# A decoder layer on one core: one norm instead of two in front of the cross layer, weights prepared two units a step, two copies on ScalarE, and the four-head norms' bias on VectorE

## The reference

```python
x = x + attn(_layernorm(x), Wqkv_w, Wqkv_b)        # 16 heads of 32, rotary, causal
x = x + xattn(_layernorm(x), ctx_2048, ...)        # self and cross, 16 heads of 128 each
x = x + ffn(_layernorm(x), w_gate_up, w_proj)      # ternary weights, silu(gate) * up, rms_norm
return x

def _layernorm(x, eps=1e-5):
    return (x - mean(x)) / sqrt(var(x) + eps)

def xattn(hidden, cond, ...):
    ln_out = _ln(hidden, ln_w, ln_b)               # (x - mu) * rsqrt(var + 1e-5) * w + b
    q  = _ln(fp8_linear(ln_out, wq),  qln_w, qln_b)    # norms over each head's 128
    k  = _ln(fp8_linear(ln_out, wk),  kln_w, kln_b)
    v  = fp8_linear(ln_out, wv)
    qx = _ln(fp8_linear(ln_out, wqx), qxln_w, qxln_b)
    kx, vx = split(cond @ w_kv_x.T);  kx = _ln(kx, kxln_w, kxln_b)
    cat = concat([gqa(q, k, v), gqa(qx, kx, vx)])      # softmax attention, 8 k/v groups
    return fp8_round(cat / proj_smooth) @ wproj.T * (proj_in_scale * proj_w_scale)
```

## Time and profile before

| | us | share of the span |
|---|---|---|
| median of 3 runs | 1264.98 | |
| the profiled execution | 1269.58 | |
| its span | 1267.8 | |
| PE busy, 6408 matmuls | 1196.8 | 94% |
| DVE busy | 947.8 | 75% |
| ACT busy | 811.6 | 64% |
| POOL busy | 608.8 | 48% |

### The profile page before, as it was taken

The page is one execution under the profiler, slowest core; times in us unless marked ns, Lnnn a source line. Parts: engine busy times, 40 slices in busy tenths (PEclk is TensorE's granted clock), DMA queues, the critical chain, the costliest instruction groups (busy, mean ns, idle before and its releaser), DMA issues.

```text
span 1267.8 us, 19453 instructions
## 1 busy us (share of the span) xinstructions
PE 1196.8 (94%) x6408; PEld 818.9 (65%) x6432; DVE 947.8 (75%) x2826; ACT 811.6 (64%) x2325; POOL 608.8 (48%) x722
## 2 busy tenths in 40 slices
PE   4999989789999999999999999999999998999998
PEld 2676666556677666676666777676677765555545
DVE  4669988999888887799999966657777877463341
ACT  4566558767877875676667765566787676652230
POOL 1728774654453454555555732124454534363370
PEclk9999889899999999999999999999999999899999
DMA  8211100012110221113233221041112100000000
GB/s 265 81 50 36 33 1 1 1 34 60 58 51 18 63 80 58 54 63 104 87 108 98 60 79 38 17 141 58 46 30 58 48 28 1 1 1 11 20 1 29
DMA packets 25461, 65.61 MB, mean 52 GB/s; under 512 B 2720, under 2 KB 8992, under 8 KB 25360
## 3 DMA queue, kind: packets, MB, share of 16 engines
q1 hardware_dynamic: 25088, 64.00, 16.4%
q10 hardware_dynamic: 272, 0.36, 0.1%
HBM read 59.37 MB, written 4.98 MB: 51 GB/s over the span
## 4 chain that ended last, share of the span: by engine, by line
PE 51%; DVE 26%; ACT 16%; POOL 4%; issue 2%; DMA 1%; SPq 0%; ACTq 0%; POOLq 0%
PE ps L869 10%; PE ps L1133 8%; PE ps L1066 7%; ACT big L799 5%; PE ps L859 5%; PE ps L1182 4%; PE ps L1028 3%; PE ps L961 3%; DVE big L412 3%; DVE big L981 2%; ACT big L964 2%; PE ps L993 2%; PE ps L500 2%; DVE big L654 2%; DVE big L240 2%
## 5 line engine op out<-in xcount | busy, mean ns | idle before, releaser
L869 PE MATMUL ps<-big 128*125 128x512 bf16 x1152 | 265.7, 380 | 0.1
L799 ACT ACTIVATE big<-ps,big 112x128 f32<-112x128 f32 (+1 forms) x512 | 192.4, 456 | 72.0 <-POOL big L429 69.6
L869 PEld LDWEIGHTS ps<-big 128*125 128x125 bf16 x1152 | 156.0, 137 | 80.7 <-issue 1.0
L428 POOL TENSOR_TENSOR big<-big 112x4 f32<-112x4 f32 (+1 forms) x128 | 39.2, 306 | 320.9 <-ACT big L423 320.8
L859 PE MATMUL ps<-big 128*112 128x512 bf16 x768 | 186.9, 387 | 5.2 <-ACT big L889 1.3
L658 POOL TENSOR_TENSOR big<-big 128x448 f32<-128x448 bf16 x96 | 103.6, 1080 | 110.2 <-DVE big L978 69.1
L859 PEld LDWEIGHTS ps<-big 128*112 128x112 bf16 x768 | 100.0, 132 | 68.6 <-issue 6.1
L981 DVE TENSOR_SCALAR big<-big 112x112 f32<-112x112 f32 (+1 forms) x256 | 132.7, 539 | 6.8
L412 DVE BATCH_NORM_STATS2 big<-ps 112x6 f32<-112x128 f32 (+1 forms) x512 | 113.3, 283 | 21.5 <-PE ps L869 19.4
L964 ACT ACTIVATE big<-ps,big 112x375 f32<-112x375 f32 x128 | 74.6, 583 | 83.9 <-DVE big L963 82.8
L1028 PE MATMUL ps<-big 125*128 125x224 f32 (+1 forms) x512 | 122.5, 362 | 4.2 <-DVE big L1010 3.4
(11 more groups left out here) (117 smaller groups left out, 2353.3 us busy)
## 6 DMA issues: line engine op xcount, KB each, us to landing
big<-in_ctx_t SPq DMA_DIRECT2D x32, 375.0 KB, 3.4
big<-in_w_s SPq DMA_DIRECT2D x16, 512.0 KB, 3.6
big<-in_w_p SPq DMA_DIRECT2D x16, 512.0 KB, 3.7
big<-in_w_x SPq DMA_DIRECT2D x16, 512.0 KB, 3.8
big<-in_w_g SPq DMA_DIRECT2D x16, 512.0 KB, 3.8
big<-in_w_d SPq DMA_DIRECT2D x8, 512.0 KB, 4.2
big<-in_w_a SPq DMA_DIRECT2D x8, 384.0 KB, 5.1
scr<-big SPq DMA_DIRECT2D x24, 128.0 KB, 1.7
```

What stands on the lines that cost most here:

```text
L799: t = act(lambda e, j=j: e.activation(z[0:rows, 128 * j:128 * j + 128], bk[0:rows, 128 * j:128 * j + 128], ACT.Identity, bias=rr[0:rows, 4 ...
L869: t = pe(lambda e, k=k, s=s, u=u, n=n: e.matmul(bk[0:CK, :], cT[:, s, k, CK * c:CK * c + CK], w[:, u, k, col:col + 512], start=n == 0, sto ...
```

## The change

Five edits:

- `l_1`, `l_1h` and their `ln_r` go. `l_0h` applies one scale that stands for both norms: the variance of the first norm's result is v/(v+e), so both together are (x - mean) / sqrt(v(1+e) + e*e), up to rounding (e = 1e-5). All later pieces of `l_` move one step forward.
- The 24 units of S0 are prepared two a step from step 4 on, so they end at step 15 instead of 27.
- `a_te` of q, and `a_s2e` of the second of four groups, go from DVE to ACT.
- The bias -mean*r of the four-head norms leaves POOL (two instructions) for DVE (one, `p_q`).
- `p_q` and `p_z` stand at the head of the next tick, lag 2, instead of inside tick 1.

```diff
-        def ln_rstd(s):
+        def ln_rstd(s, twice=False):
...
-            t = act(lambda e: e.activation(r, s["var"], ACT.Ln, bias=cf[0:rows, C_EPS:C_EPS + 1]), s["t"], t_c)
+            col, mul = (C_EPS2, 1.0 + EPS) if twice else (C_EPS, 1.0)
+            t = act(lambda e: e.activation(r, s["var"], ACT.Ln, bias=cf[0:rows, col:col + 1], scale=mul), s["t"], t_c)
...
-            tq = pool(lambda e: e.tensor_tensor(s["q"], s["mean"], r, ALU.mult), t)
-            s["tr"] = [t, pool(lambda e: e.tensor_scalar(s["q"], s["q"], -1.0, None, ALU.mult), tq)]
-            return s["i"], s["rr"], s["tr"]
+            s["te"] = t
+            return s["i"], s["rr"], None
...
+        def l_r(it):
+            it["rs"] = ln_rstd(it["st"], twice=True)
...
-            if j:
-                te = act(lambda e: e.activation(qT, src, ACT.Copy), t, of)
-            else:
-                te = dve(lambda e: e.tensor_copy(qT, src), t, of)
+            te = act(lambda e: e.activation(qT, src, ACT.Copy), t, of)
...
-            if g["c"] in (3,):
+            if g["c"] in (1, 3):
...
-        A_LEAD, A_Q, T0 = 10, 14, 34
+        A_LEAD, A_Q, T0 = 10, 13, 34
...
-                (lead + 7, ln_r),
-                (lead + 8, l_1),
-                (lead + 8, ln_r),
+                (lead + 7, l_r),
...
-                (lead + 10, l_2),
+                (lead + 9, l_2),
...
-                (lead + 8, l_1h),
...
+        def p_q(it):
+            if it["what"] != "v":
+                s = it["st"]
+                it["tr"] = [s["te"], dve(lambda e: e.scalar_tensor_tensor(
+                    s["q"], s["mean"], -1.0, s["r"], ALU.mult, ALU.mult), s["te"])]
...
+            if n >= 4:
+                next(s0prep, None)
...
-        order = [("p", 1, p_stats), ("p", 1, p_vhi), ("a", 3, t_s2), ("a", 0, t_s0), ("p", 1, p_rstd), ("a", 5, t_s4),
-                 ("p", 3, p_t), ("b", 6, b_4), ("b", 3, b_2), ("a", 1, t_s1), ("p", 1, p_z), ("a", 8, t_s6),
+        order = [("p", 2, p_q), ("p", 2, p_z), ("p", 1, p_stats), ("p", 1, p_vhi), ("a", 3, t_s2), ("a", 0, t_s0), ("p", 1, p_rstd), ("a", 5, t_s4),
+                 ("p", 3, p_t), ("b", 6, b_4), ("b", 3, b_2), ("a", 1, t_s1), ("a", 8, t_s6),
                  ("a", 4, t_s3), ("p", 0, p_mm), ("b", 2, b_m), ("b", 4, b_3), ("b", 1, b_1), ("b", 0, b_0)]
```

More of the change, by code:

```diff
@@ L29 @@
 V_WS, V_PW, V_PI, V_N = 64, 68, 69, 70
-C_ID, C_COSQ, C_SINQ, C_COSK, C_SINK, C_HALF, C_UNIT, C_EPS, C_N = (
-    0, 128, 160, 192, 224, 256, 260, 261, 262)
+C_ID, C_COSQ, C_SINQ, C_COSK, C_SINK, C_HALF, C_UNIT, C_EPS, C_EPS2, C_N = (
+    0, 128, 160, 192, 224, 256, 260, 261, 262, 263)
 K_ONE, K_DIAG, K_MASK, K_N = 0, 128, 240, 688
@@ L676, in l_0h @@
             it["l"] = (zi, z, th)
[L678 to L688, removed]
         def l_2(it):
@@ L746, in run_a @@
                 ("h", 3, a_s3),
-                (lead + 10, l_2),
[L748 to L751, removed]
+                (lead + 9, l_2),
+                (lead + 10, lambda it: l_q(it, (0,), False)),
+                (lead + 11, lambda it: l_q(it, (1,), False)),
+                (lead + 12, lambda it: l_q(it, (2,), False)),
+                (lead + 13, lambda it: l_q(it, (3,), True)),
                 (1, a_tr),
@@ L792, in p_rstd @@
                 si, rr, tr = ln_rstd(it["st"])
-                it.update(si=si, rr=rr, tr=tr)
+                it.update(si=si, rr=rr)
+        def p_q(it):
[3 more added lines that the diff above has]
+                    s["q"], s["mean"], -1.0, s["r"], ALU.mult, ALU.mult), s["te"])]
         def lnb_z(it):
@@ L1364, in _constants @@
     c[:, C_EPS] = EPS
+    c[:, C_EPS2] = EPS * EPS
     return c, d
```

## The result

| | before | after |
|---|---|---|
| median, us | 1265.59 (1264.97 to 1268.60) | 1331.27 (1328.77 to 1333.89) |
| span of the profiled execution | 1267.8 | 1327.0 |
| first cross projection on PE | 168.6 | 164.7 |
| first self scores | 214.6 | 203.5 |
| first context projection | 466.5 | 455.2 |

The changed kernel is slower by 66 us, four runs each: ratio 1.0507 [1.0482, 1.0531]. The forecast was 1251.5 with a range to 1264. From the first self scores to 489.9 us the changed kernel is 10 to 11 us ahead, about as forecast. Between the first cross-half scores and the last context projection it takes 627.2 us instead of 558.9. These 68 us, in the two cross halves, are the loss, and the forecast had charged nothing for them; less the 10 us won before, they make the 59 us by which the two profiled executions differ (the medians differ by 66).

A forecast was written before the change was run, and what follows sets the result against it. It took PE to bound the kernel in its pauseless stages and DVE from 95.04 to 174.01 us. +2.5 + 1 - 6.5 - 9.5 - 1 = -13.5 us gave 1256.1 profiled, 1251.5 median; range 1240 to 1264.

The forecast's parts named there:

- After 460: nothing: From 460 us on: no change, PE being the bound with 80 bias instructions of 0.3 us beside it; -2 to +3.
- L783 at 0.3 us: The new DVE bias instruction: 0.3 us each, taken near the lower end between 0.155 and 1.1.
- the bias meets POOL: Rival, to 460 us: L783 waits for POOL's quant instructions, 1.1 us each, 48 us on DVE; 1268.5 us, chance 0.10.
- Start, later by 2.5: 26 to 41 us: a second weight unit per step delays DVE's first bias addition and the rotary by 2.5; bounds 0.7 and 5.
- 38.50 to 88.37, later by 1: Twelve more weight units, 9 us of DVE, mostly covered by idle time: 1 us later; bounds 0 and 4.
- 88.37 to 177.56, earlier by 6.5: DVE loses about 13 us of work, PE can give 7.6: 6.5 us earlier; bounds 3 and 7.6.
- 177.56 to 206.78, earlier by 9.5: PE's hole of 5.20 and the slow clock after it mostly go: 9.5 us earlier; bounds 4 and 11.9.
- 206.78 to 460, earlier by 1: Fewer ACT waits for POOL against new bias work on DVE: 1 us earlier in all; bounds -7 and +16.
- The sum of the first attention: Start to 206.78 us: +2.5 + 1 - 6.5 - 9.5, together 12.5 us earlier.
- The doubled preparation: Two weight units a step from step 4: +3.5 us up to 88 us, eight units of 6.5 us off DVE later.
- Wrong if L783's mean is above 0.7, or PE waits for L790 in tick after tick: Signs refuting the forecast: bias mean above 0.7 us, or PE waiting for ACT's normalisation every tick from 300 us on.
- The third sign: Another sign refuting the forecast: PE's waits before 90 us exceed 5 us.

The follow-up runs named there:

- run 4: Changed kernel with the bias replaced by a one-input reciprocal at the same place on DVE (output not the layer's): 1297.55 us, ratio 1.0236.
- runs 1 to 8: The first eight follow-up kernels, all keeping the changed kernel's edits of the first attention; measured from 1252.38 to 1353.79 us.
- run 1: Changed kernel with the bias back on POOL and the normalisation back inside tick 1: 1266.17 us, ratio 0.9985 to the kernel before.
- run 2: Changed kernel with the bias back on POOL, the normalisation kept at the head of the next tick: 1260.92 us, ratio 0.9948 to the kernel before.
- run 6: Changed kernel with the one-input reciprocal as bias plus two unused POOL instructions (output not the layer's): 1266.23 us, ratio 1.0001.
- runs 1 and 3: Run 1, and the changed kernel with the bias on DVE directly ahead of the normalisation at its old place inside tick 1: 1353.79 us.
- run 7: Changed kernel with DVE's normalised probabilities ahead of the quant and ternary chains in each tick: 1290.42 us, ratio 1.0191 to the kernel before.
- run 5: Changed kernel plus two POOL instructions behind the reciprocal root whose result nobody reads: 1290.49 us, ratio 1.0182 to the kernel before.
- run 8: Run 2 with DVE's normalised probabilities ahead of the quant and ternary chains: 1252.38 us, ratio 0.9888 to the kernel before.

## Why the prediction was wrong, step by step

- **"After 460: nothing"** is the step that failed. The sentence priced 80 bias instructions at 0.3 us "beside" PE, and looked only at what they add to DVE (24 us on an engine with room). It failed three ways. The price was 0.748 in the cross halves. POOL's side of the move was never asked: removing two instructions was booked as pure gain, though the waits of before had POOL's queue standing at them for 320.8 us. And "PE is the bound" was read as safety. By total work it was: DVE had 111 us idle there. But ACT's normalisation stands behind the new instruction in every tick and holds PE's bank, so a late bias reaches PE however much idle time DVE has elsewhere (161.6 us of ACT's waits, 39 us of new idle time on PE).
- **L783 at 0.3 us**, between 0.155 and 1.1: measured 0.595 in the mean, 0.148 to 1.122 singly. Both ends were about right. The median, 0.166, is near the lower end, and the mean is not: the choice by the nearest row took the typical case for the average. L655, whose median of 277 ns spoke for the low value, has a mean of 409.
- **The rival "the bias meets POOL"** had the mechanism of run 4, and the rule of the Trainium skill beside it (page "SBUF — State Buffer", section "SBUF: two separate sides") agrees with the runs: two inputs up to 1122 ns, one input at most 180. It got 0.10, because its sum counted the 44 instructions up to 460 us and left out the 80 behind. At 0.75 each those alone would have been 60 us of DVE. Its price also came with no word on pacing, the larger half. And the row it was read from is not of its kind: L655, with its 1227 ns, has one tensor input, so that row showed that DVE and POOL collide, but not that two inputs do it. It also showed that an instruction with one input can be held up, which is what befell the probabilities.
- **Start, later by 2.5:** DVE's first bias addition was to start at 30.1 and started at 30.02; that was right. But the next rotary was late as well, and PE waited 2.36 and 1.84 us for POOL, 4.2 together where it had waited 1.35 before. The two transposes start 3.4 and 3.9 us later (34.67 and 38.52 before), above the 2.5 and under the bound of 5:

```profile
38.05 0.61 PE L543 MATMUL ps<-big 112*128 112x112 f32 x4 [2.36 <-POOL big L535]
...
42.45 0.60 PE L543 MATMUL ps<-big 112*128 112x112 f32 x4 [1.84 <-POOL big L535]
```

- **38.50 to 88.37, later by 1:** PE's idle time went from 0.07 to 2.93, of which 1.84 is the wait above. Against it stands a clock of 1.00 instead of 0.93 in this execution, 3.5 us (49.87 x 0.07) that the forecast did not contain.
- **88.37 to 177.56, earlier by 6.5:** PE is now busy in the whole stage, as forecast. The first cross projection starts 3.9 us earlier, where 2.5 + 1 - 6.5 = -3.0 was forecast, but that hit is luck, as far as the traces go. The kernels of runs 1 to 8 have the same instructions in the same order up to there, and in their traces it starts at 166.0 to 172.1, in the mean at 169.9: 1.3 later than in the one trace of before. The clock differs between these executions: from 88.37 to 159.08 PE was busy without a pause both in the changed kernel and in run 4, with 477 matmuls at 0.95 in the one and 447 at 0.88 in the other. So the early gain of 3 us is not shown.
- **177.56 to 206.78, earlier by 9.5:** the hole of 5.20 is down to 1.29, and the clock of this stage rose from 0.77 to 0.94, though one projection still ran at the lower level:

```profile
177.64 0.97 PE L615 MATMUL ps<-big 112*112 112x32 f32 x8
179.90 0.60 PE L801 MATMUL ps<-big 112*128 112x112 f32 x4 [1.29 <-ACT big L790]
180.75 3.50 PE L850 MATMUL ps<-big 128*112 128x512 bf16 x8 [0.25 <-ACT big L601]
...
186.94 1.89 PE L850 MATMUL ps<-big 128*112 128x512 bf16 x8
```

ACT's wait at the seam, the hand-over near 180 us, was 3.13 and became 1.67. The mechanism is right, the size somewhat too large. Measured from one PE instruction to the next, which the start does not disturb, the traces agree well (us):

| stretch | before | changed | run 1 | run 2 | run 6 |
|---|---|---|---|---|---|
| start to first cross projection | 168.6 | 164.7 | 166.0 | 170.9 | 170.1 |
| from there to first self scores | 46.0 | 38.8 | 42.6 | 38.8 | 39.3 |
| first self scores to first context projection | 251.9 | 251.7 | 250.2 | 248.0 | 247.8 |
| first cross-half scores to last context projection | 558.9 | 627.2 | 559.0 | 559.2 | 565.7 |

The second stretch is the seam; it gave 7 us, of 9.5 forecast. In all seven kernels with these edits and the normalisation at the head (the changed one, runs 2 and 4 to 8) it is 38.7 to 39.3; at the old place (runs 1 and 3) it is 42.6 and 41.6, so half of the gain needs the head of the tick.

- **206.78 to 460, earlier by 1:** the third stretch is 0.2 us shorter. With the bias on POOL (run 2) it is 3.7 shorter still, so the bias on DVE costs something here too.
- **The sum of the first attention** was forecast at -12.5, and the changed kernel is 11.1 us ahead at the first self scores. But 3.9 of these are the start, where the traces of runs 1 to 8 show no gain in the mean. In medians the edits bring 1.9 us at the old place (run 1) and 6.6 with the head of the tick (run 2). Single executions scatter by as much: run 1's profile is at 1261.73 where its median is 1266.17, and that of the kernel before at 1269.58 where its group's median is 1267.40, so of 7.9 us between the two traces 6.6 are the spread. The doubled preparation was forecast at +3.5 with 13 us of DVE relief behind it; by itself it costs 7.5. Why the relief of eight units L337 later gives nothing back was not separated.
- **"Wrong if L783's mean is above 0.7, or PE waits for L790 in tick after tick":** the second came true, from 490 us on, the first nearly (0.595 in the mean, 0.748 in the cross halves). The third sign, waits of PE above 5 us before 90, was just met: 2.36 and 2.93 us idle.

## What to carry to other kernels

Before taking an instruction out of a queue, look at what it waits for and what stands behind it: a queue that stands waiting may be what keeps a long instruction of that engine out of the way of another engine. Small work moved from POOL to DVE was cheap here only in the form that no POOL instruction held up (the `reciprocal` of run 4, 180 ns at most); an instruction that can be held up is priced by the mean with POOL's long instructions beside it, in every stage in which it runs and not only where the change is meant to help. And where two engines collide at a fixed place in a tick, turning round two pieces in the order may do what pacing does: run 7 and run 5 both take 1290 us, and run 7 adds no work. Last, a stage's time in one trace is one execution: where several kernels share a stage, compare their traces before calling a small gain measured.

## What the runs showed of the hardware

- A DVE instruction of four elements a row with two SBUF inputs was held up to 1122 ns beside POOL's long instructions; one with one input never took over 180 ns in 128 executions at the same place. One and the same line, L654, stayed within 611 to 619 ns with its first input in PSUM and took up to 985 with both in SBUF.
- One input is no protection in itself. The probabilities L972 (f32, SBUF to SBUF, one tensor input and a column) took 0.41 us with POOL idle and up to 1.37. Their free time suggests that they run at about double speed: 112x112 took 0.264 and 112x375 0.41, so 263 more elements cost 0.15 us, 1.8 a nanosecond, where the maximum from PSUM needs 81 ns for 73 more (0.533 at 375, 0.614 at 448), 0.9 a nanosecond (an estimate, as the operations differ). The Trainium skill, page "SBUF — State Buffer", section "Who interferes with whom", says that `tensor_scalar` can enter a mode in which it takes the pair of ports shared with GpSimd; the trace agrees: 1.22 us beside L658, 0.41 with POOL idle.
- POOL's own instructions changed less: L659 has a mean of 1286 ns after and 1166 before, L658 1059 and 1080, L369 1153 and 1227, L370 1386 and 1210. With the probabilities first L370 has 1485 (run 8), so part of the collisions falls on POOL there. In the stretches shown POOL had started first, and DVE's instruction was the one that was much longer.
- The granted clock of a stage without a pause on PE is not the same in every execution: 0.95 and 0.88 from 88.37 to 159.08 us, in two kernels with the same instructions up to there.
